# One list of stages, buffers of their own for the next image's rows, and semaphores that count per image

## The reference

```python
x = x + tanh(g_xattn[0]) * attention0(layernorm(x), ctx)      # 16 heads of 16, biases, scale 1/4
x = x + tanh(g_ffn[0])   * spectral_ffn(layernorm(x))         # a linear map (FFT, matrix, inverse FFT), bias
x = x + tanh(g_xattn[1]) * attention1(layernorm(x), ctx)      # 16 heads, relative position bias
x = x + tanh(g_ffn[1])   * mixture(layernorm(x))              # 8 experts, top 2, hidden 512, squared relu
```

## Time and profile before

| | |
|---|---|
| median of the plain runs | 2460.46 us |
| the profiled execution | 2481.56 us, its span 2479.7 us |
| mean granted TensorE clock | 0.878 |
| PE, busy | 1927.1 us, 78% |
| DVE, ACT, POOL, busy | 1047.0, 719.0, 746.0 us |
| DMA queue of SP, of GpSimd | 9.7% and 8.9% of 16 engines |

### The profile page before, as it was taken

One profiled execution on the slowest core, in us unless ns is written; L12 is line 12 of the kernel. 1 busy time (PEld: TensorE's weight loads), 2 busy tenths in 40 slices (PEclk: granted clock), 3 DMA queues, 4 the chain that ended last, 5 costly groups with the idle time before them and its releaser, 6 DMA issues.

```text
span 2479.7 us, 42311 instructions
## 1 busy us (share of the span) xinstructions
PE 1927.1 (78%) x13746; PEld 1605.5 (65%) x13747; DVE 1047.0 (42%) x2925; ACT 719.0 (29%) x1401; POOL 746.0 (30%) x1021
## 2 busy tenths in 40 slices
PE   4777777877777777877777777878770899999998
PEld 3666566656666666666666665666650688888887
DVE  2344444444444444344443444343434444444443
ACT  1222222122222222222222222222212455554554
POOL 2122322231323223231313223222313244444444
PEclk8889888988888898988888898889885899999999
DMA  2200101010100101010100101010105444444443
GB/s 83 47 27 16 33 17 25 19 31 11 31 19 22 30 16 28 17 31 13 31 19 22 28 14 33 17 25 19 28 15 169 85 70 71 72 70 71 71 70 49
DMA packets 172668, 96.99 MB, mean 39 GB/s; under 512 B 103200, under 2 KB 165792, under 8 KB 172640
## 3 DMA queue, kind: packets, MB, share of 16 engines
q1 hardware_dynamic: 144896, 58.52, 9.7%
q0 software_dynamic: 27744, 38.10, 8.9%
HBM read 44.77 MB, written 46.76 MB: 37 GB/s over the span
## 4 chain that ended last, share of the span: by engine, by line
PE 58%; issue 19%; DVE 10%; ACT 6%; POOL 4%; DMA 2%; SPq 0%; DVEq 0%; POOLq 0%; ACTq 0%
PE bank L1013 25%; PE scores L1013 9%; PE scores L1187 5%; PE bank L1074 3%; PE bank L1187 2%; ACT turned_x L713 2%; PE scores L1141 2%; DVE mx L877 2%; PE scores L1147 2%; POOL x L603 2%; PE scores L1246 2%; PE bank L1246 1%; POOL rstd L597 1%; DVE stats L831 1%; PE scores L1229 1%
## 5 line engine op out<-in xcount | busy, mean ns | idle before, releaser
L597 POOL TENSOR_TENSOR rstd<-var,half_power 128x2 f32<-128x2 f32 x128 | 90.1, 704 | 906.6 <-DVE var L837 906.6
L680 POOL DMA_INDIRECT out<-y,ids x144 | 224.5, 1559 | 356.3 <-DMA out<-y,ids 199.0
L1013 PE MATMUL bank<-w,turned_x 128*128 128x256 f32 x768 | 236.2, 461 | 85.7 <-ACT turned_x L713 85.7
L1013 PEld LDWEIGHTS bank<-w,turned_x 128*128 128x128 f32 x768 | 168.7, 231 | 131.8 <-issue 72.0
L997 DVE SCALAR_TENSOR_TENSOR h<-scores,relu 128x512 f32<-128x512 f32 x144 | 99.6, 692 | 292.2 <-ACT relu L768 244.2
L1129 PE MATMUL scores<-ident,mx 128*128 128x128 f32 x128 | 42.9, 437 | 206.7 <-DVE mx L877 206.7
L713 ACT ACTIVATE turned_x<-bank 128x512 f32<-128x512 f32 x192 | 114.7, 597 | 278.0 <-PE bank L1074 276.8
L855 DVE TENSOR_TENSOR x<-x,bank 128x512 f32<-128x512 f32 x64 | 44.0, 688 | 335.5 <-PE bank L1013 335.5
L877 DVE TENSOR_REDUCE mx<-scores 128x16 f32<-128x1232 f32 x128 | 183.9, 1436 | 4.1 <-PE scores L1120 2.4
L730 ACT ACTIVATE pr<-scores 128x1024 f32<-128x1024 f32 x128 | 124.2, 1022 | 190.5 <-PE scores L1153 190.5
L1013 PE MATMUL bank<-down_hi,ht_hi 128*128 x576 | 174.5, 303 | 0.3 <-issue 0.3
(11 more groups left out here) (200 smaller groups left out, 4525.5 us busy)
## 6 DMA issues: line engine op xcount, KB each, us to landing
xe<-sorted_rows SPq DMA_DIRECT2D x72, 257.0 KB
x<-x_rows SPq DMA_DIRECT2D x32, 256.0 KB, 2.9
out<-x_end SPq DMA_DIRECT2D x32, 256.0 KB, 3.0
raw<-w_up_t SPq DMA_DIRECT2D x8, 512.0 KB, 4.8
raw<-w_down_t SPq DMA_DIRECT2D x8, 512.0 KB, 4.8
ctx<-ctx_t SPq DMA_DIRECT2D x32, 77.0 KB, 2.0
vb<-v_rows SPq DMA_DIRECT2D x64, 38.5 KB
out<-y,ids POOLq DMA_INDIRECT x144
```

The costliest lines, as they stand in the source:

```text
L597: pool.tensor_tensor(rstd[u][:], var[u][:], half_power[:], ALU.pow).then_inc(sem(f"rstd_ready{u}"), 1)
L680: pool.indirect_dma_start(out=acc, out_offset=bass.IndirectOffsetOnAxis(ap=ids[j][:], axis=0), in_=y[j][:], in_offset=None, compute_op=ALU ...
L1013: last = pe.matmul(dst, w_, m, start=n == 0, stop=n == len(pairs) - 1)
```

## The change

Each engine still goes through one common list. It is now written out, one line per stage and engine (`one_pass`), and called three times: with only the n stages ahead of the loop, with both in it, with only the t stages behind it. In the list the stages stand as follows around the third half's `by_key_rest` and in the first pass; the rest of the loop's order on PE, ACT and DVE is the old one.

The next image's rows land in `x_new[u]`; their statistics, variance, power, normalized rows and turned rows have buffers of their own (`mv0`, `var0`, `rstd0`, `xs`, `turned_s`); GpSimd writes x[u] as x_new plus bias. `x_end` is one per image. The counts of semaphores are per image (`added{u}`, `mx_ready{u}`, `pr_ready{u}` and so on), and `hold` and `clear` keep the stage's own count. Some stages get waits that they had not.

```diff
@@ the order
+            run("load_x", n, 0)
+            run("load_x", n, 1)
+            run("tables", first)
...
+            run("less_max", t, 0, 1)
+            run("exp", t, 0, 1, 0)
+            run("exp", t, 0, 1, 1)
+            run("turn", t, "t1", 1)
+            run("turned", t, "t1", 1)
+            run("keys", n, 0)
+            run("keys_hi", n, 0)
+            run("keys_lo", n, 0)
+            run("by_key_rest", t, 0, 1)
+            run("exp_rest", t, 0, 1)
+            run("rows_by", t, 1, 1)
+            run("add_x", t, 1, 1)
+            run("stats", t, 2, 1)
+            run("rstd", t, 2, 1)
+            run("norm", t, 2, 1)
+            run("sums", t, 0, 1, 0)
...
+            run("norm", t, 3, 0)
+            run("bias_x", n, 0, 0)
+            run("stats", n, 0, 0)
+            run("rstd", n, 0, 0)
+            run("spread", n, 0, 1)
...
+            run("turn_start", n, 0)
+            run("turned_start", n, 0)
+            run("values", n, 0)
+            run("value_rows", n, 0)
+            run("values_out", n, 0)
...
+            run("queries", n, 0, 0)
@@ SP
-            def load_x(u, t):
-                wait(sp, f"var_ready{u}", num(t, 4, 0))
-                sp.dma_start(x[u][:], a["x_rows"][bass.ds(num(t, 2 * T, u * T), T), :]
+            def load_x(t, u):
+                wait(sp, f"xs_ready{u}", num(t, 1, 0))
+                carrier(sp)
+                wait(sp, f"x_biased{u}", num(t, 2, -1))
+                carrier(sp)
+                sp.dma_start(x_new[u][:], a["x_rows"][bass.ds(num(t, 2 * T, u * T), T), :]
...
+                sp.wait_ge(sem(f"added{u}"), num(t, 3, 3))
@@ GpSimd
+            def bias_x(t, s, u):
+                if s == 0:
+                    pool.wait_ge(sem(f"x_in{u}"), num(t, 16, 16))
+                    wait(pool, f"added{u}", num(t, 3, 0))
+                else:
+                    pool.wait_ge(sem(f"xn_ready{u}"), num(t, 3, 1))
+                pool.tensor_tensor(x[u][:], (x_new, x)[s][u][:], (bo_row, ffn_row)[s][:, None, :].to_broadcast([P, NC, D]), ALU.add)\
+                    .then_inc(sem(f"x_biased{u}"), 1)
...
+                        wait(pool, f"sc_done{u}", num(t, 2, l - 1))
                         wait(pool, f"rest_done{u}", num(t, 2, l - 1))
@@ ACT
-            def queries(u, t, l):
+            def queries_hi(t, u, l):
                 act.wait_ge(sem(f"q_done{u}"), num(t, 2, l + 1))
+                wait(act, f"sc_done{u}", num(t, 2, l))
+                wait(act, f"rest_done{u}", num(t, 2, l))
...
+            def exp(t, u, l, n):
                 scale = DH ** -0.5 if l == 0 else 1.0
+                act.wait_ge(sem(f"sc_done{u}"), num(t, 2, l + 1))
+                wait(act, f"pv_done{u}", num(t, 2 * NC, l * NC))
+                act.activation(pr[u][:, 2 * n:2 * n + 2].rearrange("p j g t -> p (j g t)"),
...
+            def exp_rest(t, u, l):
+                scale = DH ** -0.5 if l == 0 else 1.0
+                act.wait_ge(sem(f"rest_done{u}"), num(t, 2, l + 1))
+                wait(act, f"pv_done{u}", num(t, 2 * NC, l * NC))
@@ DVE
+            def norm_start(t, u):
+                dve.wait_ge(sem(f"rstd0_ready{u}"), num(t, 1, 1))
+                wait(dve, f"turned_s{u}", num(t, 1, 0))
+                for c in range(NC):
+                    last = dve.tensor_scalar(xs[u][:, c], x_new[u][:, c], mv0[u][:, c, 0:1], rstd0[u][:, c:c + 1], ALU.subtract, ALU.mult)
+                last.then_inc(sem(f"xs_ready{u}"), 1)
...
-                    wait(dve, f"x_out{1 - u}", num(t, 16, 16 * u))
+                    wait(dve, f"x_out{u}", num(t, 16, 0))
...
+                if l == 0:
+                    wait(dve, f"turned{u}", num(t, len(TURNS), 0))
                 link(dve.reciprocal(rden[:, c], o[:, :, DH]), t)
@@ PE
+            def turn_start(t, u):
+                pe.wait_ge(sem(f"xs_ready{u}"), num(t, 1, 1))
+                transposes(xs[u]).then_inc(sem(f"turned_s{u}"), 1)
+                hold("A", f"s_ready{u}", t, 1, 1)
...
                 pe.wait_ge(sem(f"kr_ready{l}"), num(t, 4, 4))
-                clear("rest", t)
+                pe.wait_ge(sem(f"q_lo_ready{u}"), num(t, 2, l + 1))
+                pe.wait_ge(sem(f"neg_mx_ready{u}"), num(t, 2, l + 1))
+                clear("rest")
...
-                    pe.wait_ge(sem("scores_read"), so_far("scores", t))
-                    clear("C", t)
-                else:
-                    clear("rest", t)
+                pe.wait_ge(sem(f"pr_ready{u}"), num(t, 4, 2 * l + 2))
+                if c == 1:
+                    pe.wait_ge(sem(f"pr_rest_ready{u}"), num(t, 2, l + 1))
+                clear(("C", "rest")[c])
```

More of the change, by code:

```diff
@@ L149, in build @@
         xn = [sb1(f"xn{u}", [P, NC, D]) for u in range(2)]
-        x_end = sb1("x_end", [P, NC, D])
+        x_new = [sb1(f"x_new{u}", [P, NC, D]) for u in range(2)]
+        xs = [sb1(f"xs{u}", [P, NC, D]) for u in range(2)]
+        x_end = [sb1(f"x_end{u}", [P, NC, D]) for u in range(2)]
         xr = sb1("xr", [P, NC, D])
@@ L261, in wait @@
                 engine.wait_ge(sem(name), value)
-        def since(t, per, value):
-            return value if isinstance(t[0], int) else t[0] * per + value
-        made = {}
         held = {}
[L272 to L333, removed]
-        def part1_order(do, fori):
[L337 to L347, removed]
-            held.clear()
[L349 to L383, removed]
-            with fori(0, PAIRS - 1) as it:
[L385 to L389, removed]
-                do["store_x"](0, t)
-                fourth_half(t, True)
-                do["load_x"](1, n)
-                do["store_x"](1, t)
-                first_half(n, send_steps(0, t), router_steps(1, t), choose_steps(1, t))
-                second_half(n, send_steps(1, t))
-                assert all(made[what] - before[what] == each for what, each in EACH.items()), (made, before)
-            for what, each in EACH.items():
-                made[what] += (PAIRS - 2) * each
-            for name, (signal, per, value) in held.items():
-                held[name] = signal, per, value + (PAIRS - 2) * per
-            t = (PAIRS - 1, 0)
-            third_half(t, False)
-            do["store_x"](0, t)
-            fourth_half(t, False)
-            do["store_x"](1, t)
-            for slot in steps(send_steps(0, t), router_steps(1, t), choose_steps(1, t)).values():
-                for stage, *args in slot:
-                    do[stage](*args)
-            for stage in ("weigh", "places", "send"):
-                do[stage](1, t)
@@ new lines, in part1_order, with run @@
+        def part1_order(do, fori):
+            def run(stage, t, *args):
+                if t is not None and stage in do:
+                    do[stage](t, *args)
+            held.clear()
+            one_pass(run, None, (0, 0), (0, 0))
+            with fori(0, PAIRS - 1) as it:
+                rebased(it)
+                before = counts(0)
+                one_pass(run, (it, 0), (it, 1), None)
+                assert counts(1) == before, (before, counts(1))
+            rebased(PAIRS - 2)
+            one_pass(run, (PAIRS - 1, 0), None, None)
@@ L694, in _, with bias @@
             act.wait_ge(sem("consts"), 13)
-            def bias():
+            def bias(first):
                 act.wait_ge(sem("tab_in"), TABLES)
@@ L752, in weigh @@
                 last.then_inc(sem(f"routed_ready{u}"), 1)
-            part1_order({"bias": bias, "keys": keys, "turn": turn, "queries": queries, "turn_max": turn_max,
-                         "exp": exp, "gate": gate, "weigh": weigh}, act.Fori)
+            part1_order({"bias": bias, "keys_hi": keys_hi, "turned_start": turned_start, "turned": turned, "queries_hi": queries_hi,
+                         "max_turned": max_turned, "exp": exp, "exp_rest": exp_rest, "gate_exp": gate_exp, "weigh": weigh}, act.Fori)
             for n in range(2 * E):
@@ L940, in _ @@
             part1_order({
[L941 to L943 removed]
+                "bias": bias, "keys_lo": keys_lo, "stats": stats_of, "norm_start": norm_start, "norm": norm, "add_x": add_x,
+                "value_rows": value_rows, "queries_lo": queries_lo, "maxima": maxima, "divide": divide, "choose": choose,
+                "columns": columns, "places": places,
             }, loop)
```

431 lines of the change are left out of this document (295 added, 136 removed).

## The result

The changed kernel takes 2483.45 us (median of four runs, 2481.57 to 2484.50) against 2460.39 us before: a ratio of 1.0096, with a 95% interval of 1.0078 to 1.0113. It is slower by 23 us, 1%. The prediction had 2503 us, 20 us too much, with 2483 inside its range. The profiled execution took 2484.50 us, its span 2482.7.

What follows compares the result with a forecast made beforehand. PE was taken as the bound, in a strictly serial order with 26 us idle a pass; 30 (move) + 15 (waits) - 2 (first pass) = +43 us on the 2460.46 us median gave 2503 us, range 2478 to 2532.

Steps and rivals of the forecast that it cites:

- The move: Third half on PE: keys ahead of by_key_rest makes turn t2 2.0 us a pass later, 30 us in 15 turns.
- Its first part: Third half on PE: keys waits for ACT's copy, so rows_by starts at 799.25 instead of 796.60.
- the 5.71 us: Time from rows_by to turn t2 in the last pass, without keys between, taken for the changed loop instead of 6.38.
- SP and POOL are not involved: Claim that moving keys in the loop takes only its ACT and DVE parts along.
- The added waits: Extra semaphore waits on ACT, at queries_hi and first exp, cost 1.0 us a pass, 15 us in the loop.
- rival (b): Added waits are free, taken by the sequencer while it waits anyway; only the move counts: 2488 us, chance 0.20.
- 4 x 2: Two added waits at each of four queries_hi a pass, 0.09 us each: 0.72 us a pass.
- Rival (a): PE's clock falls behind the new wait, 1.5 us a pass on top, +22: 2525 us, chance 0.20.
- The load of x: Next image's load no longer waits for the last statistics; already hidden behind the gate's matmuls, so counted zero.
- rival (d): DVE's wait for x sets the next image's start; all 34.7 us go: 2426 us, faster, chance 0.05.
- Rival (c): Moving keys costs nothing, its idle time being the old one shifted; only waits remain: 2473 us, chance 0.06.
- The first pass: values(0) ahead of the first queries, first power before the second spread: 2 us gained once, from 0 to 3.7.

Runs made afterwards that it cites:

- e2: The kernel before with one edit, keys of the next pair in slot 3 instead of slot 4 of the third half: 2484.26 us, ratio 1.0108.
- e1: The changed kernel with keys, keys_hi and keys_lo of the next pair put back behind the normalization of t2: 2457.30 us, 0.9988 of the kernel before.
- e0: The kernel before, unedited, profiled a second time: 2460.12 us, ratio 0.9999.
- e4: The changed kernel with keys put back and without the waits added on ACT: 2431.68 us, 0.9884 of the kernel before.
- e5: The changed kernel with keys(n, 0) moved in front of turn_max of the third half: 2434.8 us (runs 2430.81 to 2446.83), 0.9915 of the kernel before.
- e10: e5 without the waits added on ACT: 2456.35 us, 0.9977 of the kernel before.
- e3: The changed kernel without ACT's added waits, two in queries_hi and one in each exponential: 2482.95 us, 1.0090 of the kernel before.
- e6: The changed kernel with GpSimd's spread of layer 0 waiting for the normalization of t2: 2487.79 us, 1.0109 of the kernel before.
- e7: e1 with two small, unneeded ACT copies ahead of the copy of turn t1: 2448.02 us, 0.9953 of the kernel before.
- e8: e1 with six small, unneeded ACT copies ahead of the copy of turn t1: 2479.43 us, 1.0061 of the kernel before.
- e11: e10 with keys(n, 1) also moved in front of turn_max, in the first half: 2389.29 us, 0.9702 of the kernel before.

## Why the prediction was right and wrong

**The move.** Right in place and sign, and in the wait that it foresaw: e2 alone gives the loss, e1 without it gives it back. Its first part was right to 0.02 us (2.67 measured). The step that failed is the one that carried the 5.71 us of the earlier trace rows over to a pass that has `keys`. The last pass of part 1 has no `keys` and so no spread on GpSimd behind the power; in the changed pass there is one, since the spread waits for `keys_lo`. The row was taken from a place where the neighbour on another engine was missing, and "SP and POOL are not involved" was wrong for POOL. It was 6.58, with 0.76 of the difference from the normalization, 1.49 us against 0.73. The Trainium skill, SBUF — State Buffer, section "Who interferes with whom", has this as a rule: DVE and GpSimd share a pair of ports, `tensor_scalar` can take both, and the one that issues second is blocked until the first has finished. The trace agrees in the order and the size: the normalization's two instructions start 0.07 and 0.11 us behind kb_hi and kb_lo, take 0.78 and 0.79 us instead of 0.41, and each ends 0.15 us after the one that it started behind. How much of each stands still within its 0.78 us, the records don't show. In idle time the term was 2.7 us a pass instead of 2.0.

**The added waits.** The term that was most mis-sized: 1.0 us a pass, 15 us in all, against 0.13 us in the wait for q_hi and at most another 0.1 at the exponentials. Not the price was wrong (0.13 us for two waits, where the earlier trace rows gave 0.09 for each), but the count: "4 x 2" for q_hi was one times two. The other six waits were run as well, but ahead of the wait that came last. So rival (b) had this term nearly right and for the reason that it gave, a sequencer that takes them while it waits in any case; it fails only where the added waits stand behind the late one. The place of the Trainium skill, VectorE: DVE Perf Modes, section on the DRAIN you can't avoid, that the prediction set beside this rival is about semaphores signalled after an instruction, not about waits; no run here tests it.

**The clock.** Rival (a) let it take another 1.5 us a pass; it gave back 1.0. Behind the longer waits the matmuls are slow at other places: the biases of the scores by key became fast and the second group of sums slow. Over 12 passes, e0:

```profile
L1141 PE MATMUL scores<-bias_hi,ident_r 128*128 128x512 f32 x96 | 55.9, 582 | 0.0
...
L1187 PE MATMUL scores<-vb,pr 128*128 128x136 f32 x768 | 96.9, 279 | 0.0
```

and after (busy us, mean ns):

```profile
L1254 PE MATMUL scores<-bias_hi,ident_r 128*128 128x512 f32 x96 | 39.7, 413 | 0.0
...
L1305 PE MATMUL scores<-vb,pr 128*128 128x136 f32 x768 | 110.7, 304 | 0.0
```

413 ns against 582 there, 304 against 279 here. The prediction called itself wrong if the pass stayed at 112.7 us, and it did; it compared with the first profile, whose clock was the lower one. Against e0 the pass is longer by 1.71 us: 2.70 of waits less 1.00 of clock. No term of the sum stood for that 1.00, since the forecast held the clock fixed.

Nor are the two independent parts. Nine of the thirteen traces fall on three lengths:

| 12 passes, us | traces | PE idle, us per pass |
|---|---|---|
| 1310.70, 1310.73 | e4, e5 | 26.44, 27.00 |
| 1331.18 to 1331.19 | e0, e1, e10 | 26.77, 26.53, 26.31 |
| 1351.57 to 1351.69 | before (first profile), after, e2, e3 | 26.80, 29.47, 29.54, 29.44 |

(e6 has 1358.25, e7 1324.17, e8 1350.85, e11 1279.96.) Within a line the matmuls' busy time makes up what the idle time differs by, to about 0.01 us a pass. e10 waits less than e4 and is 20.5 us longer. What the move did is to add 2.70 us of idle time and to take the loop from the second length to the third, and the first profile of before made that same step with no idle time added. That the loss is 1.71 us a pass, and not 2.7, follows from no price of a wait.

**The rest.** The load of x was hidden, as said: in e1, with x_new and its own buffers, DVE has no wait for x left, where before had 34.7 us, and the kernel is only 3 us faster, all of it ahead of the loop; rival (d) is out. Rival (c), with the move free, is out by e2. DVE's busy time grew by 19 us in 12 passes and nothing came of it beyond the term above; 9 of the 19 are in e1 as well. The first pass gained 3 us in e1 (158.52 against 161.61), where 2 were taken from a range of 0 to 3.7.

**Together.** The 45 us for the move and the waits became 26 us (an estimate, 1.71 x 15; e1 measures as much), nearly all of it the move's, which alone measures 24 us (e2); the -2 of the first pass became -3. That makes 23 us, as measured. Of the forecast's excess of 20 us, about 13 come from the count of the waits, 15 from the clock, for which it had no term, and 1 from the first pass; against that the move's idle time was about 10 us more than forecast. That the forecast came so near is in part luck: errors of opposite sign cancelled, and the steps of the pass's length were not foreseen at all.

What stays open: why the clock falls at one place of a pass and not at another, and why the loop keeps to a few lengths. The runs show that both move by small edits; none lets one foretell where to.

## What to carry to other kernels

A stage that writes a shared bank cost here what PE then stood for, not its own length; put it where PE waits in any case, as in e11. When a duration is borrowed from another place of the trace, check what the other engines did beside it there, and see in the trace whether an added wait stands ahead of the late one, where it cost nothing, or behind it. In a kernel with waits of some microseconds, split every difference into PE idle and PE busy over the same work before it is explained, look at single passes as well as at their mean, and profile the base more than once.

## What the runs showed of the hardware

The same kernel had its loop at 112.63 and at 110.93 us a pass with equal idle time (26.80 and 26.77 us), and within one execution its passes alternated between 109.46 and 112.40 us at granted clocks of 0.89 and 0.86, again with equal idle time. 12 passes took 1310.7, 1331.2 or 1351.6 us within 0.1 in nine of thirteen traces, with up to 2.7 us a pass between the idle times on one length. An edit that changed the idle time by 0.09 us a pass moved the kernel by 1% (e1 to e4), and added work made it faster (e7). Taking the same waits out changed the time by nothing, -26 us or +22 us, by what stood around them (e3, e4, e10). Effects of one stage, measured alone, don't add in such a kernel: an edit has to be measured in the version in which it will stay. Two added semaphore waits cost ACT 0.13 us where they stood behind the wait that ended last, and nothing in the three places where they stood ahead of it.
